# A 7x7 convolution on normalised images: a prologue with empty matmuls, and the moments of the first units moved to fixed places

## The reference, cut to what matters

```python
def _gn(v, G=32, eps=1e-05):                 # 32 channels, 32 groups: one mean and variance per image and channel
    g = v.reshape(B_, G, C_ // G, H_, W_)
    m = jnp.mean(g, axis=(2, 3, 4), keepdims=True)
    s = jnp.var(g, axis=(2, 3, 4), keepdims=True)
    return ((g - m) / jnp.sqrt(s + eps)).reshape(v.shape)

def construct_kernel(weight, P):             # 9 weighted points per channel pair, spread bilinearly over a 7x7 filter
    ...
    for di, dj, frac in corners:
        kern = kern.at[:, cidx, ih + di, iw + dj].add(weight * frac[None], mode='drop')
    return kern

# x: (32, 32, 56, 56) float32, weight: (32, 32, 9), P: (2, 32, 9), bias: (32,)
x = x + conv_7x7(_gn(x), construct_kernel(weight, P), padding=3) + bias[None, :, None, None]
```

## Time and profile before

| | us |
|---|---|
| median of 2 runs (320.38 to 321.65) | 321.01 |
| the profiled execution | 321.43 |
| its span, first to last instruction | 319.6 |
| busy PE / DVE / ACT / POOL | 288.1 / 266.9 / 225.1 / 177.8 |
| mean granted TensorE clock | 0.956 |

### The profile page before, as it was taken

The page is one execution under the profiler, slowest core; times in us unless marked ns, Lnnn a source line. Parts: engine busy times, 40 slices in busy tenths (PEclk is TensorE's granted clock), DMA queues, the critical chain, the costliest instruction groups (busy, mean ns, idle before and its releaser), DMA issues.

```text
span 319.6 us, 9702 instructions
## 1 busy us (share of the span) xinstructions
PE 288.1 (90%) x3436; PEld 201.4 (63%) x3436; DVE 266.9 (84%) x358; ACT 225.1 (70%) x327; POOL 177.8 (56%) x339
## 2 busy tenths in 40 slices
PE   4930699799999999999999999999999899999990
PEld 2710466567666677777766777777777577776760
DVE  5359598999898999999998989999999799996221
ACT  2259897878878796969696978888787769570300
POOL 6342646656565849393948566565657392934000
PEclk9585599999999999999999999999999999999997
DMA  8952445979999898989999979999998949498605
GB/s 143 156 108 58 119 134 116 245 181 213 224 211 241 185 251 168 264 177 240 196 235 199 258 162 229 224 220 229 216 237 183 251 98 229 104 236 221 131 2 102
DMA packets 128255, 59.09 MB, mean 185 GB/s; under 512 B 122068, under 2 KB 122068, under 8 KB 128228
## 3 DMA queue, kind: packets, MB, share of 16 engines
q1 hardware_dynamic: 115204, 24.90, 42.0%
q0 software_dynamic: 9312, 33.04, 39.1%
q10 hardware_dynamic: 3712, 0.80, 1.4%
HBM read 12.88 MB, written 12.85 MB: 81 GB/s over the span
## 4 chain that ended last, share of the span: by engine, by line
PE 70%; DMA 5%; POOL 5%; issue 1%; DVE 1%; DVEq 0%; ACT 0%; POOLq 0%
PE ps_eo L796 22%; PE ps_x L796 17%; PE ps_s L796 17%; PE ps_y L796 13%; DMA xb<-xs 5%; POOL xn L704 2%; POOL xb L673 1%; PE ps_stat L741 1%; DVE xs L457 1%; POOL rtmp L679 1%; DVE result L461 1%; POOL rtmp L681 0%; DVEq L54 0%; ACT rinv L320 0%; DVE var L431 0%
## 5 line engine op out<-in xcount | busy, mean ns | idle before, releaser
L673 POOL DMA_DIRECT2D xb<-xs x192 | 94.1, 496 | 55.6 <-DVE xs L457 52.6
L796 PE MATMUL ps_eo<-xs,w 128*64 128x392 f16 (+1 forms) x576 | 98.7, 324 | 0.0
L796 PE MATMUL ps_eo<-xb,w 128*64 128x392 f16 (+1 forms) x576 | 98.7, 324 | 0.0
L796 PEld LDWEIGHTS ps_eo<-xb,w 128*64 128x64 f16 x576 | 61.6, 109 | 18.3
L796 PE MATMUL ps_s<-xb,w 128*64 128x392 f16 (+1 forms) x384 | 69.9, 332 | 3.1 <-DMA xb<-xs 3.1
L796 PE MATMUL ps_s<-xs,w 128*64 128x392 f16 (+1 forms) x384 | 70.4, 332 | 0.1
L796 PE MATMUL ps_x<-xb,w 128*64 128x392 f16 x384 | 67.7, 328 | 0.0
L796 PE MATMUL ps_x<-xs,w 128*64 128x392 f16 x384 | 67.7, 328 | 0.0
L344 ACT ACTIVATE xs<-e 128x900 f16<-128x900 f32 x48 | 59.4, 1238 | 11.3 <-DVE e L434 8.8
L796 PEld LDWEIGHTS ps_eo<-xs,w 128*64 128x64 f16 x576 | 61.7, 109 | 7.2
L457 DVE TENSOR_TENSOR xs<-e,xs 128x900 f16<-128x900 f32 x48 | 64.8, 1349 | 0.1
(11 more groups left out here) (90 smaller groups left out, 450.5 us busy)
## 6 DMA issues: line engine op xcount, KB each, us to landing
xb<-xs POOLq DMA_DIRECT2D x96, 168.8 KB, 4.2
xb<-xs POOLq DMA_DIRECT2D x96, 166.9 KB, 4.6
xraw<-x SPq DMA_DIRECT2D x124, 98.0 KB, 3.0
out<-result SPq DMA_DIRECT2D x124, 98.0 KB, 4.5
xraw<-x ACTq DMA_DIRECT2D x4, 98.0 KB, 4.0
out<-result ACTq DMA_DIRECT2D x4, 98.0 KB, 3.7
wnat<-L_conv_weight POOLq DMA_DIRECT2D x1, 36.0 KB, 3.5
pts<-L_conv_P POOLq DMA_DIRECT2D x2, 1.1 KB, 2.9
```

Source lines behind the costliest of these rows:

```text
L673: pool.dma_start(dst[32 * g:32 * g + 32, 0:run - line * past], src[32 * f:32 * f + 32, line * past:run]).then_inc(shifted[par][b], DMA)
L796: last = pe.matmul(into[p:p + HALF, :, 0:PER * wide], w[:, n // 2, s, q, t, :], moving.rearrange("p n q m -> p n (q m)"), start=fresh and ...
```

## The change

Statistics: `fold` is dropped and `eye` used in its place, so the sums are folded unscaled; the factor goes into DVE's `mean` and `spread`. `negmean` gets two buffers. POOL builds `eye` with narrower selects. The first image of unit 0 has its own semaphore, and ACT sums it before the second has come.

TensorE's prologue: after the transposed weights five empty matmuls; the mean fold of unit 0 before the first chunk, its variance fold before the second, the scales before the third; then six empty matmuls, the mean fold of unit 1, six more. The variance fold of unit 1 moves into unit 0 before stream 2, the mean fold of unit 2 before stream 3, its variance fold before stream 8. In later units a mean fold also waits for the variance of the unit before.

ACT takes the filter products out of PSUM instead of DVE. ACT and DVE get written-out orders for units 0 and 1 up to their steps for unit 1. POOL's Newton step is apart from `normalise`; in unit 0 the third shift goes between them, in unit 1 the second. The last stores wait for each half of the last output.

```diff
-        negmean = sb("negmean", [128, PER], fp32)
+        negmean = sb("negmean", [128, 2, PER], fp32)
...
-            queue.wait_ge(combined, OUTS * UNITS)
             for m in range(PER):
+                queue.wait_ge(combined, OUTS * UNITS - 1 + m)
...
-        FILTER_OF = (1, 2, 2, 4, 3, 3, 4, 5, 5)
+        FILTER_OF = (1, 2, 2, 3, 4, 4, 3, 5, 5)
...
             def sums(u, r, nth):
-                act.wait_ge(x_loaded[r], LOAD * (nth + 1))
-                if not isinstance(u, int) or u > 0:
+                if isinstance(u, int) and u == 0:
+                    act.wait_ge(first_image, LOAD // PER)
+                else:
+                    act.wait_ge(x_loaded[r], loaded(r, nth))
                     act.wait_ge(folded, mean_fold(u - 1))
                 for m in range(PER):
+                    if m and isinstance(u, int) and u == 0:
+                        act.wait_ge(x_loaded[r], loaded(r, nth))
...
+            def take_filters(t):
+                act.wait_ge(kern_in_psum, 2 * t + 2)
+                act.wait_ge(scales_ready, 1)
+                act.activation(kern[:, :, :, t, :].rearrange("p j q (r o) -> p r (j q) o", r=2),
+                               (ps_eo, ps_x)[t][:, :, 0:256].rearrange("p r (v o) -> p r v o", o=CH),
+                               ACT.Copy, scale=scales[:, 0:1]).then_inc(kern_ready, 1)
...
+            take_filters(0)
+            take_filters(1)
             act.wait_ge(edges_zeroed, 2)
             high(0, 0, *BATCHES[0], first=True)
+            high(0, 0, *BATCHES[1], first=True)
             filter_high(0)
             filter_high(1)
-            high(0, 0, *BATCHES[1], first=True)
             sums(1, 1, 0)
             filter_high(2)
+            sums(2, 2, 0)
+            high(0, 0, *BATCHES[2], first=True)
+            high(0, 0, *BATCHES[3], first=True)
+            squares(1, 1)
+            act.wait_ge(bias_loaded, DMA)
+            middle(0, first=True)
+            high(0, 0, *BATCHES[4], first=True)
+            root(1)
             filter_high(3)
+            high(0, 0, *BATCHES[5], first=True)
+            seed(0, 0, 0, first=True)
+            normalise(1, 1, first=True)
             filter_high(4)
...
+            seed(0, 0, 1, first=True)
+            high(1, 1, *BATCHES[0], first=True)
+            high(1, 1, *BATCHES[1], first=True)
+            squares(2, 2)
+            sums(3, 3, 0)
+            high(1, 1, *BATCHES[2], first=True)
+            root(2)
+            high(1, 1, *BATCHES[3], first=True)
+            normalise(2, 2)
+            high(1, 1, *BATCHES[4], first=True)
+            high(1, 1, *BATCHES[5], first=True)
+            for h in range(1, RING):
+                step(h, h, (h + 3) // RING, True, True, True)
...
-                dve.wait_ge(newton, NEWTON * u)
-                dve.tensor_copy(negmean[:, :], mean_ps).then_inc(negmean_ready, 1)
+                if not isinstance(u, int) or u > 1:
+                    dve.wait_ge(newton, NEWTON * (u - 1))
+                dve.tensor_scalar(negmean[:, par], mean_ps, -1.0 / (SIDE * SIDE), None, ALU.mult
+                                  ).then_inc(negmean_ready, 1)
...
+            odd_differences(0, 0)
             dve.wait_ge(kern_ready, 2)
             filter_sum(0, sums4[:, 0:2], kern[:, 0::2], kern[:, 1::2])
-            filter_sum(1, sums4[:, 2:4], kern[:, 0:2], kern[:, 2:4])
             dve.wait_ge(filt_summed, 1)
             filter_sum(2, sums4[:, 4:5], sums4[:, 0:1], sums4[:, 1:2])
-            odd_differences(0, 0)
+            filter_sum(1, sums4[:, 2:4], kern[:, 0:2], kern[:, 2:4])
+            low(0, 0, *BATCHES[0])
+            low(0, 0, *BATCHES[1])
+            filter_low(0)
             differences(0, 0)
-            low(0, 0, *BATCHES[0])
-            filter_low(0)
-            low(0, 0, *BATCHES[1])
+            mean(1, 1)
+            second_differences(0, 0)
+            low(0, 0, *BATCHES[2])
             filter_low(1)
-            second_differences(0, 0)
+            low(0, 0, *BATCHES[3])
             second_differences(0, 2)
...
+            filter_low(2)
             spread(1)
...
+            low(0, 0, *BATCHES[4])
+            filter_low(3)
+            low(0, 0, *BATCHES[5])
+            outs_0(0)
+            mean(2, 0)
+            outs_1(0)
+            odd_differences(1, 1)
+            filter_low(4)
+            low(1, 1, *BATCHES[0])
+            low(1, 1, *BATCHES[1])
+            outs_2(0, 0, 0)
+            differences(1, 1)
+            spread(2)
+            second_differences(1, 0)
+            low(1, 1, *BATCHES[2])
+            low(1, 1, *BATCHES[3])
+            outs_3(0)
+            second_differences(1, 2)
+            low(1, 1, *BATCHES[4])
+            low(1, 1, *BATCHES[5])
+            step(1, 1, 0, True, True)
...
+            newton_step(0)
             normalise(0)
             for u in range(UNITS):
                 shift(u, u % 2, 0)
                 if u == 0:
                     shift(u, u % 2, 1)
                 if u + 1 < UNITS:
+                    newton_step(u + 1)
+                if u == 0:
+                    shift(u, u % 2, 2)
+                if u == 1:
+                    shift(u, u % 2, 1)
+                if u + 1 < UNITS:
                     normalise(u + 1)
+                if u > 1:
+                    shift(u, u % 2, 1)
                 if u:
-                    shift(u, u % 2, 1)
-                shift(u, u % 2, 2)
+                    shift(u, u % 2, 2)
...
+            for n in range(5):
+                pe.matmul(ps_x[:, n % 2, 0:N], zeros[:, 0:128], zeros[:, 0:N], start=True, stop=True)
...
                 pe.wait_ge(negmean_ready, u)
+                if not isinstance(u, int) or u:
+                    pe.wait_ge(var_ready, u)
                 fold_columns(PER, 2 * PER)
...
-                if k == CHUNKS - 1:
-                    pe.wait_ge(fold_built, 1)
-                    pe.wait_ge(wmax_ready, 1)
+                if k == 0:
+                    pe.wait_ge(eye_built, 2 * GROUPS)
                     mean(0)
+                if k == 1:
+                    variance(0)
+                if k == 2:
+                    pe.wait_ge(srow_step, 7)
+                    pe.matmul(ps_s[:, 128:131], ones[:, :], srow[:, 2:5], start=True, stop=True
+                              ).then_inc(scales_in_psum, 1)
...
-            for k in range(2):
-                last = pe.matmul(ps_x[:, k, 0:N], zeros[:, 0:128], zeros[:, 0:N], start=True, stop=True)
+            for n in range(6):
+                mark(n)
+            mean(1)
+            for n in range(6):
+                last = mark(n)
             last.then_inc(marked, 1)
-            mean(1)
-            variance(1)
...
+                    if first:
+                        if s == 2:
+                            variance(1)
+                        if s == 3:
+                            mean(2)
+                        if s == 8:
+                            variance(2)
+                    elif stats:
+                        if s == 1:
+                            mean(u + 2)
+                        if s == 5:
+                            variance(u + 2)
```

More of the change, by code:

```diff
@@ L99, in build @@
         eye = sb("eye", [128, 128], fp32)
-        fold = sb("fold", [128, 128], fp32)
         own = sb("own", [CP, CH], fp32)
@@ L313, in squares @@
                 for m in range(PER):
-                    last = act.activation(junk[:, r % 2, m, :], image(r, m), ACT.Square, bias=negmean[:, m:m + 1],
+                    last = act.activation(junk[:, r % 2, m, :], image(r, m), ACT.Square, bias=negmean[:, r % 2, m:m + 1],
                                           accum_out=ssq[:, m:m + 1])
@@ L355, in seed @@
                 if first:
-                    act.wait_ge(marked, k + 1)
+                    act.wait_ge(marked, 1)
                 else:
@@ L503, in step @@
                 if stats:
-                    mean(u + 2)
+                    mean(u + 2, h)
                 if nxt:
@@ L726, in _ @@
             for n in range(8):
-                last = pe.matmul(ps_y[:, n % 2, 0:N], zeros[:, 0:128], zeros[:, 0:N], start=True, stop=True)
-            last.then_inc(marked, 1)
+                pe.matmul(ps_y[:, n % 2, 0:N], zeros[:, 0:128], zeros[:, 0:N], start=True, stop=True)
             pe.wait_ge(weights_loaded, DMA)
@@ L809, in step @@
                         pe.wait_ge(m11_ready, u + 1)
-                    if s == 1 and stats:
-                        mean(u + 2)
-                    if s == 5 and stats:
-                        variance(u + 2)
+                    if first:
[10 more added lines that the diff above has]
+                            variance(u + 2)
                     if s == 4:
```

67 lines of the change are left out of this document (23 added, 44 removed).

## The result

The changed kernel takes 326.16 us (median of 325.82 and 326.51), the kernel before 321.01 (320.38 to 321.65): a ratio of 1.0164, interval 1.0112 to 1.0215. It is slower by 1.6%, which is outside the predicted range. The profiled execution took 325.82, its span is 324.0 against 319.6, so the span holds the whole of the difference between the profiled executions (+4.4).

A forecast was written before the change was run, and what follows sets the result against it. TensorE, busy nine tenths of the span, was taken as the bound, from unit 2 just ahead of a DVE, ACT and POOL loop. 321.43 - 1.6 + 1.0 - 0.5 = 320.3, corrected to 319.5; range 315 to 322.5.

The forecast's parts named there:

- The statistics of unit 0: Prologue: variance of unit 0 at 12.95 against 18.12, normalised image at 17.4 instead of 23.1.
- The first streams: DVE's work for unit 0: low parts of streams 0 to 2 done at 22.4, unit 0 starting at 27.5, 7.3 earlier.
- The loop: DVE, ACT and POOL from unit 2 on: variance to landed copy 11.9 us, with TensorE 0.9 us or less ahead.
- The wait that the change puts in DVE's queue: DVE inside unit 0: stands from 30.0 for the variance fold of unit 1 at 31.5, unit 0's last low parts behind it.
- The copy ahead of normalising: POOL: third shifted copy of unit 0, 0.6 to issue and 1.95 for four DMAs, before normalising unit 1, done at 39.5.
- The tail: Last stores: the first two of each queue wait for half of the last output instead of both, 0.5 gained.
- the lead of unit 0: Unit 0's start 7.3 us earlier: all but 1.6 given back in stalls in units 0, 1 and 2.
- the gain of 1.6: Middle third of unit 2: its second copy lands at 77.5, against 79.11 before.
- The step that failed first: Filter matmuls: with the clock rising at 14.9 as before, they end at 18.1 and the filter is ready at 18.9.
- the slower rival: Filter: folds interrupt the matmuls, clock stays at 1.2 GHz, 2.2 later, plus 1.0 in unit 0: 322.7, chance 0.2.
- the term for unit 0's start: Clock loss in unit 0's first matmuls: taken as 1.0 us, between nothing lost and 1.95 as before.
- The correction of 0.8 to the median: Sum: 320.3 lowered to 319.9, the profiled execution lying 0.4 above the median, then 0.4 for waits priced too long: 319.5.

The follow-up runs named there:

- e1_dense: Kernel after with more empty matmuls in TensorE's prologue (at the start, ahead of and behind the filter, around the mean fold of unit 1): 321.22 us, 0.9993.
- e7_folds_back: Kernel after with the variance fold of unit 0 and the scales back behind the three thirds of the filter matmuls: 328.02 us, 1.0183.
- e12_dense_front: Kernel after with denser empty matmuls only ahead of the filter (16 and 9 instead of 8 and 5): 322.56 us, 1.0024.
- e9_halves: Kernel after keeping its prologue, empties and split last stores, but with old orders and fold places from the first low parts on: 320.60 us, 0.9968.
- e10_halves_dense: Kernel after with old orders from the first low parts on, plus denser empty matmuls (16, 9, 8, 16, 26): 314.86 us, 0.9781.
- e3_pool_first: Kernel after with POOL normalising unit 1 ahead of the third shifted copy of unit 0: 327.22 us, 1.0205.
- e4_var_first: Kernel after with unit 1's variance folded ahead of unit 0, its root on ACT right behind its squares, middle output last: 325.01 us, 1.0140.
- e6_dense_var_pool: Kernel after with denser empties, unit 1's variance folded ahead of unit 0, POOL normalising unit 1 before the third copy, unit 2's variance a stream earlier: 319.60 us, 0.9961.
- e2_no_empty: Kernel after without the empty matmuls the change added (four stay behind the mean fold of unit 1): 326.23 us, 1.0179.
- e11_halves_dense_var: Kernel after with old orders from the first low parts, denser empties, and DVE's variance of unit 1 ahead of unit 0's last two low parts: 316.02 us, 0.9801.

## Why the prediction was wrong

**What held.** The statistics of unit 0: variance within 0.65, normalised image within 0.24. The first streams: from filter to low parts 3.4 (predicted 3.5), from there to the landed copy 5.4 (5.1). The loop: in the kernel after the chain of waits runs from DVE's variance of unit 3 over POOL and a copy to the middle third of unit 2 once more, 71.95 to 84.23, 12.3 against the 11.9 taken from the earlier trace rows, so that a delay upstream arrives in the time whole. The wait that the change puts in DVE's queue was there, though longer: 3.82 in front of the variance of unit 1 (30.0 to 31.5 predicted). The copy ahead of normalising: 41.03, then 43.14. The tail: 0.6 won (0.5).

That the lead of unit 0 would be eaten in units 0 and 1 was right as well, and e1_dense shows it with the filter at the high clock: from the variance of unit 1 to that of unit 3 its landmarks lie 0.5 to 1.3 behind the predicted ones, though its first copy came 1.4 ahead. But the gain of 1.6 that was to be left at the middle third of unit 2 is not there either (79.83, predicted 77.5).

**The step that failed first** is in the filter: "second third 12.9 to 15.7 if the clock rises at 14.9 as before, scales 0.4, last third 2.0, so 18.1". The clock did not rise. The second third ran from 13.48 to 17.26 and the last from 17.70 to 21.48; the filter was ready 3.3 late. The condition was taken from a row whose stretch had no fold in it: in the earlier trace rows TensorE is busy for 6.60 of 6.83 up to 14.90 with the filter alone, the mean fold of unit 0 came only in front of the last third. The change puts a fold and the scales between the thirds, and e7_folds_back shows that these are what keeps the clock down. TensorE's timeline in the kernel before has that fold at

```profile
15.18 0.28 PE L741 MATMUL ps_stat<-moments,fold 128*64 128x2 f32 x4
```

The clock had risen at 14.9, ahead of it. The mechanism stood in the text as the slower rival, with a chance of 0.2; no row spoke against that rival, since none showed a rise across a fold.

**The second** is the term for unit 0's start. I put 1.0, half of the 1.95 of the earlier trace rows, for want of a nearer row. The clock was low until 34.76, from the first copy at 31.03 that is 3.7 us at half speed, a loss of 1.9: the upper bound. The row that was nearest, 0.98 us of work in 4.2 ahead of the fall, spoke for it. In the kernel after the clock had not been up since 7.46, so its empties (six from 22.27, 2 us of waiting, six from 26.68) had nothing to hold; e12_dense_front has the same six and six behind a high clock, which falls at 19.70, in the wait of 2.94 between them, and unit 0's first matmuls take 0.53. The Trainium skill, "TensorE: Matmul & The Clock Gate", section "HAM oscillation — how this bites in real kernels", has bursts of matmuls with waits between them start at the low clock; that fall agrees.

**The third** is small: the steps between the variance of unit 1 and the middle third of unit 2 took 47.2 (37.07 to 84.23) where I had 46.0 (31.5 to 77.5). No step of them was off by more than 0.4, but nearly all in one direction. In the working, the way from the low parts to the landed copy, 0.6 + 1.5 + 3.2, makes 5.3 and not 5.1 (measured 5.4), and the last unit, 294.73 to 311.51, is 16.78 and not 16.75; neither decides anything.

Sum on the profiled execution: 320.3 forecast, +3.5 to unit 0's copy (3.3 of it the filter), +2.1 to the variance of unit 1 less the 1.0 already in the sum, +1.1 down to unit 2: 326.0; measured 325.82. The correction of 0.8 to the median went the wrong way too: the profiled execution lay 0.3 under it.

The slower rival was priced at 3.2 over the forecast and cost 6.7. Its bound "3.5 each for the second and third part" was about right (3.8 each), but it was counted from a second third that had started 0.6 earlier, and unit 0's start was priced as in the forecast plus 1.0; it lacked the third point and the wrong correction. So the range ended just under the price of a rival that was itself 3.5 too cheap.

**Where the stalls were off.** TensorE stood 2.25 in unit 1 for the middle output, predicted 4.3; 1.76 for the third copy of unit 0 (46.80) and 2.67 for the first of unit 1 (54.66), where the prediction had delays of 1 to 2; in unit 2 it stood for less than the 2 predicted (idle 0.56 in 75.00 to 84.20). It came later itself, and behind the stands of 2.67 and 2.25 the clock fell again, at 55.24 and at 65.48. That these waits cost nothing beside the loop is likely, as DVE waits for no matmul there, but no run takes them out alone.

**The parts of the price.** By the runs, against the kernel after: the clock 4.9 us (5.5; e1_dense), most of it in the filter (e12_dense_front, 3.6 or 4.5); the fixed order of units 0 and 1 5.6 us (6.3; e9_halves), the clock that falls in its waits included; both together 11.3 (12.3; e10_halves_dense), near their sum. The change itself is a prologue that is worth 3.0 (3.8) where the clock allows it, and pays both prices.

What stays open: what unit 0's start would win at the high clock in the new order, and which of the fixed places costs how much of the 5.6. Moving single ones (e3_pool_first, e4_var_first, e6_dense_var_pool) gave −1.1, 1.2 and 0.2 by the medians, and in each trace another place took over; the places were only undone all at once.

## What to carry to other kernels

A small matmul put into a dense stretch of TensorE can cost the rise of the clock that the stretch would have brought, as it did here: before moving a fold forward, look whether the granted clock rose inside the stretch that it will split. Then either bring the clock up ahead of the stretch by empties that are dense up to it (e12_dense_front), or leave the fold out of it (e7_folds_back). Where a chain through several engines sets the pace, work that is moved to a fixed place inside another engine's order makes one queue wait for the other; take such places back together, as here each one alone handed the wait on. An empty matmul is worth something only where the durations of the matmuls behind it show that the clock is up.

## What the runs showed of the hardware

**Two small matmuls among dense ones, and the clock did not rise.** In the kernel after TensorE was busy for 13.46 of 14.00 us, with empties, a mean fold and the filter, the variance fold of 0.38 and the scales of 0.58 among its thirds, and stayed at 1.2 GHz; in e9_halves 13.80 of 13.80 with the same result by its durations. In e7_folds_back, without the two between the thirds, it rose at 16.24; in the kernel before at 14.90, ahead of the only fold among them (15.18). Where the clock was up before the filter, the same fold and scales did not bring it down: in e1_dense and e12_dense_front, up from 6.1 and 6.0, all three thirds take 1.03 to 1.13 a row.

**The record can show a clock that the work does not have.** e9_halves has in its windows:

```profile
6.20:20.00 13.80, 13.80 (x45) 9.54 (x45) 5.40 (x18) 5.88 (x12) 5.16 (x17) 1.00 0.92 155
```

that is 1.00, while its rows of four passes take 2.07, as at 0.50. The clock's record of that run has its first entry at 39.56, that of e2_no_empty at 35.52 and that of e7_folds_back at 16.24, and ahead of it the windows show 1.00. This may be why the two runs of the kernel after record mean clocks of 0.943 and 0.984 for 325.82 and 326.51 us. The duration of a known matmul is the better witness.

**POOL and DVE slow each other.** Normalising 32 partitions takes 2.13 in the kernel after (43.14), where DVE idles, and 3.00 in e3_pool_first (39.32), where it moved beside a low part and outputs on DVE; as in the earlier trace rows. A product of two columns went from 0.19 to 1.01 beside a low part of DVE (e11_halves_dense_var). So a step of POOL that moves changes its price with its neighbours.
